# Transposing pairs of 16-bit integers as fp32 words in phase 2 of a decoder layer

## The reference, cut to what matters

```python
def _act_quant(x):
    scale = 127.0 / jnp.clip(jnp.max(jnp.abs(x), axis=-1, keepdims=True), EPS)
    xq = jnp.clip(jnp.round(x * scale), -128.0, 127.0) / scale
    return x + jax.lax.stop_gradient(xq - x)
...
def _bitlinear(x, w):
    return jnp.einsum('bsh,oh->bso', _act_quant(x), _weight_quant(w))
gate = jax.nn.silu(_bitlinear(x, w_gate))
up = _bitlinear(x, w_up)
return _bitlinear(gate * up, w_down)
...
x = _layernorm(x + _L0_attn_ref(x, L0_attn_w_q, L0_attn_w_k, L0_attn_w_v, L0_attn_w_out), axis=-1)
x = _layernorm(x + _L0_xattn_ref(x, ctx_4096, L0_xattn_weight), axis=-1)
x = _layernorm(x + _L0_ffn_ref(x, L0_ffn_w_gate, L0_ffn_w_up, L0_ffn_w_down), axis=-1)
```

## Time and profile before

| | us |
|---|---|
| three runs | 1411.53, 1415.58, 1416.80 |
| median | 1415.58 |
| the profiled execution's own time | 1411.78 |
| its span | 1410.0 |
| phase 2, from the first L717 at 850.98 | 559 |
| one turn of the loop in phase 2 | 34.4 |

### The profile page before, as it was taken

One profiled execution on the slowest core, in us unless ns is written; L12 is line 12 of the kernel. 1 busy time (PEld: TensorE's weight loads), 2 busy tenths in 40 slices (PEclk: granted clock), 3 DMA queues, 4 the chain that ended last, 5 costly groups with the idle time before them and its releaser, 6 DMA issues. The chain is left out here.

```text
span 1410.0 us, 23306 instructions
## 1 busy us (share of the span) xinstructions
PE 1365.8 (97%) x7560; PEld 690.9 (49%) x7560; DVE 1056.1 (75%) x1851; ACT 623.7 (44%) x1209; POOL 217.0 (15%) x262
## 2 busy tenths in 40 slices
PE   8889999999999999999999989999999999999996
PEld 3344555545545554554554544444444444444443
DVE  4996456446577777868867768888888888888884
ACT  7876474455455545545544542332222232223221
POOL 0003213121131321312222221000000000000000
PEclk9999999999999999999999999999999999999999
DMA  9515454445435354453443583222222222222200
GB/s 375 223 61 181 137 186 143 168 132 182 142 111 177 137 160 141 147 178 113 159 159 124 134 278 111 76 75 74 74 74 74 74 74 74 74 74 74 77 27 16
DMA packets 63732, 178.92 MB, mean 127 GB/s; under 512 B 15392, under 2 KB 26832, under 8 KB 63696
## 3 DMA queue, kind: packets, MB, share of 16 engines
q1 hardware_dynamic: 63696, 178.48, 39.2%
HBM read 153.02 MB, written 25.43 MB: 127 GB/s over the span
## 5 line engine op out<-in xcount | busy, mean ns | idle before, releaser
L512 PE MATMUL ps<-weights,xT 128*128 128x512 f16 x2112 | 472.7, 381 | 7.0 <-ACT v L776 6.3
L512 PEld LDWEIGHTS ps<-weights,xT 128*128 128x128 f16 x2112 | 204.4, 98 | 243.1 <-issue 14.2
L717 PE MATMUL ps<-weights 128*128 128x512 fp8e4 (+1 forms) x1536 | 300.0, 357 | 0.0
L717 PEld LDWEIGHTS ps<-weights 128*128 128x128 bf16 x1536 | 146.7, 98 | 155.0
L512 PE MATMUL ps<-weights 128*128 128x512 f16 x768 | 168.9, 379 | 1.1 <-DVE weights L1165 0.6
L745 PE MATMUL ps<-weights 128*128 128x512 fp8e4 x704 | 157.9, 381 | 0.0
L972 ACT ACTIVATE weights<-ps,xscale 128x512 f32<-128x512 f32 x96 | 61.7, 643 | 175.7 <-PE ps L717 175.7
L832 ACT ACTIVATE prob<-prob,negmax,undo 128x128 f32<-128x128 f32 x256 | 122.7, 482 | 8.1 <-DVE negmax L1197 8.0
L512 PEld LDWEIGHTS ps<-weights 128*128 128x128 f16 x768 | 74.9, 98 | 91.8 <-DVE weights L1165 1.6
L745 PEld LDWEIGHTS ps<-weights 128*128 128x128 bf16 x704 | 67.8, 98 | 76.5 <-issue 1.1
L1529 POOL TENSOR_TENSOR rstd<-rstd,expo 128x1 f32<-128x1 f32 x32 | 17.8, 557 | 524.5 <-DVE rstd L1094 524.5
(11 more groups left out here) (162 smaller groups left out, 1791.0 us busy)
## 6 DMA issues: line engine op xcount, KB each, us to landing
wch<-w_ffn SPq DMA_DIRECT2D x96, 688.0 KB, 4.3
wch<-sim_scratch SPq DMA_DIRECT2D x96, 128.0 KB
ternary_scratch<-tern SPq DMA_DIRECT2D x48, 172.0 KB, 1.9
ctx<-ctx SPq DMA_DIRECT2D x16, 512.0 KB
wo_raw<-x_scratch SPq DMA_DIRECT2D x16, 512.0 KB, 3.3
out<-k SPq DMA_DIRECT2D x16, 512.0 KB, 2.7
x_in<-xT_in SPq DMA_DIRECT2D x15, 512.0 KB, 6.9
weights<-x SPq DMA_DIRECT2D x15, 512.0 KB, 10.7
```

Source lines behind the costliest of these rows:

```text
L512: ins = nc.tensor.matmul(ps[:, bank], partsT[:, a, t], weights[:, t, w, half * HALF:(half + 1) * HALF], start=(t == 0 and a + w == 0), sto ...
L717: ins = nc.tensor.matmul(ps[:, 2 * w + a, 0:n], xqT[:, t], w8m[:, t, at:at + n], start=(t == 0), stop=(t == KT - 1))
```

## The change

- The integers are held in fp16 with 512 added (`LIFT`), so that two of them side by side are an fp32 word; the subtraction of 512 and the clip at -128 are done in the copy out of PSUM.
- Two neighbouring columns are transposed together as one fp32 word: `xq_T` issues 4 transposes of 128x128 fp32 in place of 8 in bf16, those of h are 11 in place of 22. They use `idf`; `idb` and its copy at the start are gone.
- A transposed word holds the values of columns 2p and 2p+1 in one place, so the weights are loaded with two neighbouring rows of the matrix in one partition (`gate8_pairs`, `up8_pairs`, `down8_pairs`). The matmuls themselves are as before.
- The copies from PSUM take the even and then the odd halves of the words: they read 16-bit elements with a step of two and write `xqT` and `hT` without gaps.
- The transposes of h go to three banks (4, 5 and 3) in groups of 4, 4 and 3 words' tiles, so that none waits for a bank of its own turn; there are three copies, of 1024, 1024 and 768 elements, in place of 768, 768, 640 and 640. The down product waits for the first at tile 0, for the second at tile 8 and for the third at tile 16.

```diff
-HT_USES = ((0, 6), (6, 12), (12, 17), (17, 22))
-HQ_NEEDS = [-(-min(hi * P, I) * 4 // I) for _, hi in HT_USES]
+JT = IT // 2
+LIFT = 512.0
+HT_USES = ((0, 4), (4, 8), (8, JT))
+HQ_NEEDS = [-(-min(hi * 2 * P, I) * 4 // I) for _, hi in HT_USES]
...
-        TH, AC = 4, 6
+        TH, AC = (4, 5, 3), 6
...
-                    for m, w8m in enumerate((gate8, up8)):
-                        src = tern_dram[m * WCH:(m + 1) * WCH].rearrange("r p n -> (r p n)").rearrange("(k p n) -> p k n", p=P, n=I)
-                        for t in (0, 4):
-                            sp.dma_start(w8m[:, t:t + 4].bitcast(U8), src[:, t:t + 4]).then_inc(ffn_in, 16)
+                    for m, w8m in enumerate((gate8_pairs, up8_pairs)):
+                        src = tern_dram[m * WCH:(m + 1) * WCH].rearrange("r p n -> (r p n)").rearrange("(j p m) -> p j m", p=P, m=2 * I)
+                        for j in (0, 2):
+                            sp.dma_start(w8m[:, j:j + 2].bitcast(U8), src[:, j:j + 2]).then_inc(ffn_in, 16)
...
-                bank = ps[:, 2].bitcast(BF16)
-                for t in range(KT):
-                    ins = nc.tensor.transpose(bank[:, t * P:(t + 1) * P], xq[:, t * P:(t + 1) * P], idb[:])
+                for j in range(KT // 2):
+                    ins = nc.tensor.transpose(ps[:, 2, j * P:(j + 1) * P], rope_c[:, j * P:(j + 1) * P], idf[:])
...
                 for u, (lo, hi) in enumerate(HT_USES):
-                    w = u % 2
-                    if not (isinstance(i, int) and i == 0 and u < 2):
-                        pe.wait_ge(trh_free[w], i * 2 + u // 2)
                     pe.wait_ge(hq_ready, i * 4 + HQ_NEEDS[u])
...
-                    if t in (0, 12):
-                        for w in range(2):
-                            pe.wait_ge(trh_free[w], i * 2 + (1 if t == 0 else 2))
-                        apart(pe)
+                    for u, (lo, _) in enumerate(HT_USES):
+                        if t == 2 * lo:
+                            pe.wait_ge(trh_free[u], i + 1)
+                            apart(pe)
...
-                nc.vector.tensor_scalar(xq, xrnd, MAGIC, 127.0, ALU.subtract, ALU.min).then_inc(xq_ready, 1)
+                nc.vector.tensor_scalar(xq, xrnd, MAGIC - LIFT, 127.0 + LIFT, ALU.subtract, ALU.min).then_inc(xq_ready, 1)
...
-                nc.vector.tensor_scalar(xqT, ps[:, 2].bitcast(BF16).rearrange("p (t n) -> p t n", n=P), -128.0, None,
+                src = ps[:, 2].bitcast(F16).rearrange("p (j n e) -> p j e n", n=P, e=2)
+                nc.vector.tensor_scalar(xqT.rearrange("p (j e) n -> p j e n", e=2), src, LIFT, -128.0, ALU.subtract,
                                         ALU.max).then_inc(pair_free[1], 1)
...
-                    src = ps[:, TH + w].bitcast(BF16)[:, 0:(hi - lo) * P].rearrange("p (t n) -> p t n", n=P)
-                    nc.vector.tensor_scalar(hT[:, lo:hi], src, -128.0, None, ALU.max).then_inc(trh_free[w], 1)
+                    dve.wait_ge(trh_full[u], i + 1)
+                    src = ps[:, TH[u]].bitcast(F16)[:, 0:(hi - lo) * 2 * P].rearrange("p (j n e) -> p j e n", n=P, e=2)
+                    dst = hT[:, 2 * lo:2 * hi].rearrange("p (j e) n -> p j e n", e=2)
+                    nc.vector.tensor_scalar(dst, src, LIFT, -128.0, ALU.subtract, ALU.max).then_inc(trh_free[u], 1)
```

More of the change, by code:

```diff
@@ L95, in decoder @@
         idf = sb("idf", [P, P], F32)
-        idb = sb("idb", [P, P], BF16)
         expo = sb("expo", [P, 2, 9], F32)
@@ L128, in decoder @@
         down8 = w8[:, 2 * KT * I:2 * KT * I + IT * D].rearrange("p (k n) -> p k n", k=IT)
+        gate8_pairs = w8[:, 0:KT * I].rearrange("p (j m) -> p j m", j=KT // 2)
+        up8_pairs = w8[:, KT * I:2 * KT * I].rearrange("p (j m) -> p j m", j=KT // 2)
+        down8_pairs = w8[:, 2 * KT * I:2 * KT * I + IT * D].rearrange("p (j m) -> p j m", j=JT)
         hbuf = over(over_out, I)
-        hq = over(over_out, IT * P // 2).bitcast(BF16)
+        hq_pairs = over(over_out, IT * P // 2)
+        hq = hq_pairs.bitcast(F16)
         hT = over(over_out, IT * P // 2).bitcast(BF16).rearrange("p (t n) -> p t n", n=P)
@@ L189, in decoder @@
         xres_last = wo_raw[:].rearrange("p a n -> p (a n)")[:, D + 2:2 * D + 2]
-        xq = rope_c[:].bitcast(BF16)
+        xq = rope_c[:].bitcast(F16)
         xrnd = xT[:].rearrange("p a t n -> p (a t n)").bitcast(F32)
@@ L281, in decoder @@
         hq_ready = sem("hq_ready")
-        trh_full = [sem("trh_full0"), sem("trh_full1")]
-        trh_free = [sem("trh_free0"), sem("trh_free1")]
+        trh_full = [sem(f"trh_full{u}") for u in range(len(HT_USES))]
+        trh_free = [sem(f"trh_free{u}") for u in range(len(HT_USES))]
         var2_ready = sem("var2_ready")
@@ L431, in turn @@
                         sp.wait_ge(pj_full[w], pj_uses(B - 1, 5) + 1)
-                    for m, w8m in enumerate((gate8, up8)):
-                        src = tern_dram[m * WCH:(m + 1) * WCH].rearrange("r p n -> (r p n)").rearrange("(k p n) -> p k n", p=P, n=I)
-                        for t in (0, 4):
-                            sp.dma_start(w8m[:, t:t + 4].bitcast(U8), src[:, t:t + 4]).then_inc(ffn_in, 16)
[L436 to L441, removed]
+                    for m, w8m in enumerate((gate8_pairs, up8_pairs)):
+                        src = tern_dram[m * WCH:(m + 1) * WCH].rearrange("r p n -> (r p n)").rearrange("(j p m) -> p j m", p=P, m=2 * I)
+                        for j in (0, 2):
+                            sp.dma_start(w8m[:, j:j + 2].bitcast(U8), src[:, j:j + 2]).then_inc(ffn_in, 16)
+                    src = tern_dram[2 * WCH:3 * WCH].rearrange("r p n -> (r p n)").rearrange("(i m) -> i m", m=2 * D)
+                    full = (JT - 1) * P
+                    src_j = src[0:full].rearrange("(j p) m -> p j m", p=P)
+                    for lo, hi in ((0, 3), (3, 7), (7, JT - 1)):
+                        sp.dma_start(down8_pairs[:, lo:hi].bitcast(U8), src_j[:, lo:hi]).then_inc(ffn_in, 16)
+                    sp.dma_start(down8_pairs[0:I // 2 - full, JT - 1].bitcast(U8), src[full:I // 2]).then_inc(ffn_in, 16)
                 if has_next and not has_next2:
@@ L726, in turn2 @@
                 for u, (lo, hi) in enumerate(HT_USES):
-                    w = u % 2
-                    if not (isinstance(i, int) and i == 0 and u < 2):
-                        pe.wait_ge(trh_free[w], i * 2 + u // 2)
                     pe.wait_ge(hq_ready, i * 4 + HQ_NEEDS[u])
[L731 to L734, removed]
+                    for j in range(lo, hi):
+                        ins = nc.tensor.transpose(ps[:, TH[u], (j - lo) * P:(j - lo + 1) * P], hq_pairs[:, j * P:(j + 1) * P], idf[:])
+                    ins.then_inc(trh_full[u], 1)
                 if not (isinstance(i, int) and i == 0):
@@ L1422, in _ @@
             dve.wait_ge(const_in, 64)
-            nc.vector.tensor_copy(idb[:], idf[:]).then_inc(set_up, 1)
             first_rope(0)
@@ L1471, in turn2 @@
                         st.wait(s)
-                    nc.vector.tensor_scalar(hquarter(a, hq), hquarter(a), MAGIC, 127.0, ALU.subtract, ALU.min) \
+                    nc.vector.tensor_scalar(hquarter(a, hq), hquarter(a), MAGIC - LIFT, 127.0 + LIFT, ALU.subtract, ALU.min) \
                         .then_inc(hq_ready, 1)
                 for u, (lo, hi) in enumerate(HT_USES):
-                    w = u % 2
                     if u == 2 and has_next:
@@ L1547, in turn @@
                     pool.wait_ge(sims_ready, b)
-                    nc.gpsimd.memset(down8[64:P, IT - 1], 0.0).then_inc(padded, 1)
+                    nc.gpsimd.memset(down8_pairs[I // 2 - (JT - 1) * P:P, JT - 1], 0.0).then_inc(padded, 1)
                     pool.wait_ge(padded, 1)
```

1 line of the change is left out of this document (removed).

## The result

The changed kernel takes 1435.54 us (median of 4 runs, 1433.80 to 1435.97) against 1413.81 of before (4 runs, 1411.53 to 1416.80): ratio **1.0153, interval 1.0138 to 1.0168**, so 1.5% slower and clear of the noise. The profiled execution took 1435.39 us with a span of 1433.6, 23.6 more than the span of before. Phase 2 begins at 851.20 (850.98 before), so the loss lies in phase 2.

What follows compares the result with a forecast made beforehand. PE sets the pace, and DVE's chain from h to x has no slack. Fifteen turns at +1.42 us give +21.3, the last turn -0.3, sum +21.0: 1432.8 from the profiled execution, 1436.6 from the median; forecast 1435, range 1430 to 1442.

Steps and rivals of the forecast that it cites:

- What bounds: Phase 2 turn of 34.40 us: PE busy 34.08, waiting before the down product and for the next block's x.
- The chain: DVE from the integers of h to those of x: two slower copies +1.32 us, third +0.07, PE's transposes of x +1.39.
- The copy's time: DVE copies from PSUM at a step of two: 1.21 us for 1024 elements, 0.95 us for 768.
- Start of the down product: One slow copy in place of two fast ones: first weights at 1116.14 against 1116.18, nothing won.
- The new waits: Down product at tiles 8 and 16: second and third copies done 2.4 and 1.9 us before PE needs them.
- Behind the chain: From the transposes of x to the next gate matmul: copy's slack used up, 0.2 us more, turn +1.42 us.
- The transposes of x: Four fp32 transposes take 0.44 us against 0.59 for eight bf16 ones, saving 0.15 us of PE on the path.
- The last turn: Only the first copy precedes the down product, which starts at 1391.32 against 1391.61: -0.3 us.
- The signs: Profile after: 1024-element copies about 1210 ns, turn 35.8 us, PE idle about 1.4 us before transposes of x, clock 1.00.
- The copies keep two elements a step: Rival at L1481 and L1150: copies of 0.691 and 0.55 us, about 1411, or 1408 to 1417 us; chance 0.09.
- The clock: Rival: a 1.4 us wait each turn lowers PE's clock, 36 us more, 1469 us; chance 0.03.
- Slower still: Rival: a copied element takes more than one step, 1.79 us a copy, 3.6 a turn, 1466 us; chance 0.03.

Runs made afterwards that it cites:

- the new order: Kernel before with bf16 transposes, three banks and DVE's copies of h moved to where DVE waits: 1408.82 us, ratio 0.9964.
- tried alone: Kernel before with bf16 transposes and plain copies, groups of 8, 8 and 6 tiles in three banks, down product waiting group by group: 1414.14 us.
- the run that counted on it: Changed kernel with plain copies and the new order, 1407.37 us, compared with the new order on bf16 transposes, 1408.82 us.
- the kernel with plain copies: Changed kernel with all copies of h and x without gaps, PE's weight loads taking the step of two: 1414.27 us, ratio 1.0007.
- the kernels with copies of 4.8 us: Changed kernel with copies reading without gaps and writing SBUF in scattered pieces: rows of two elements 1667.54 us, rows of four 1668.85 us.

## Why the prediction was right, point by point

- **What bounds.** PE sets the pace and waits at two places, of which the second, DVE's chain from the integers of h to those of x, has no slack. Right, and shown twice: lengthening it lengthens the turn, and shortening it (the new order) makes the kernel before faster. "No slack" is 0.20 us too strict: it compared L1146 with the load at 1124.24, but the matmuls of the transposes started at 1124.44. The chain is 1.43 us longer, the matmuls came 1.24 later.
- **The copy's time.** 1.21 us taken, 1.220 to 1.224 measured; 0.95 and 0.948 for 768. The number held, but its argument did not, and that it held is luck: with plain reading and a step on the writing side the words are read once, and the copy takes 1.29 us. The price of 1024 words read and that of one element a step happen to be the same.
- **Start of the down product.** Nothing won: +0.02 us. One slow copy takes what two fast ones took.
- **The new waits.** Covered, as the sum had it, and without cost when tried alone.
- **The chain.** +1.39 forecast, +1.43 at L1146. The third copy put L1099 0.86 us behind it, 0.87 forecast.
- **Behind the chain.** +1.42 in all forecast, 1.55 to 1.57 measured. The term most at fault is the lag behind the copy of x: its end (1137.51 + 1.22 = 1138.73) to the first gate matmul (1138.88) is 0.15 us, where 0.06 were taken. Behind L1146 the lag is 0.06 here too (1136.75 to 1136.81), so it was carried over from a place where it holds to one where it doesn't; why it is longer there stays open. It makes 1.4 us in fifteen turns, and with the chain's 0.04 it is the whole 2 us that the turns fell short. DVE still waited 0.23 us for L1489, where none was forecast; nothing hung on it.
- **The transposes of x.** "Saves 0.15 us of PE" is wrong. The 0.59 us for eight in the earlier trace rows were read from weight loads, which ran ahead while matmuls of the down product were still going; on PE itself eight in bf16 take 0.45 and four in fp32 0.44. The copy did start 0.15 us earlier behind the first load, but because PE was idle when the load came. A right shift for a wrong reason; the run that counted on it (3 to 4 us for pairs) missed.
- **The last turn.** -0.3 forecast. From the integers to the first load of the down product it took 3.00 us (1414.96 - 1411.96) against 3.26 (1391.61 - 1388.35), so -0.26 there. But nothing of it arrived: from the same integers to the end of the down product it is 13.97 us against 13.93, and to the end of the span 21.64 against 21.65. In both kernels PE comes out of a wait of 3.7 us or more, and the granted clock is 0.50 in the two microseconds from 1415 and from 1391. In the changed kernel the loads go at their slow spacing of 0.43 us until 5.54 us behind the integers, before until 5.07. 0.47 us more at half the clock cost about as much as the earlier start had won. The rows after, then before:

```profile
1411.96 1.79 DVE L1472 TENSOR_SCALAR weights<-weights 128x688 f16<-128x688 f32 x4
...
1414.96 0.14 PEld L745 LDWEIGHTS ps<-weights 128*128 128x128 bf16 x2 [0.82 <-issue]
1414.99 10.94 PE L745 MATMUL ps<-weights 128*128 128x512 fp8e4 x44 [0.57 <-issue]
...
1417.50 7.93 PEld L745 LDWEIGHTS ps<-weights 128*128 128x128 bf16 x37 [0.28 <-issue]
```

```profile
1388.35 1.79 DVE L1472 TENSOR_SCALAR weights<-weights 128x688 bf16<-128x688 f32 x4
...
1391.71 10.57 PE L745 MATMUL ps<-weights 128*128 128x512 fp8e4 x44
...
1393.42 8.36 PEld L745 LDWEIGHTS ps<-weights 128*128 128x128 bf16 x39 [0.28 <-issue]
```

- **The total.** 1435 forecast, 1435.54 measured, and that they agree this closely is luck too. The spans of the profiled executions differ by 23.6 us, where 21.0 were forecast: the turns were 0.13 us short each, and the last turn gave nothing. The medians differ by 21.7.
- **The signs.** Copies of 1210 ns were named, 1220 to 1224 came; a turn of 35.8 us, 35.95. Of PE's idle time about 1.4 us were forecast ahead of the transposes of x; there are 1.09 there and 0.60 ahead of the down product. The sum does not name the latter, but it only takes the place of the third and fourth group of transposes.
- **The rivals.** "The copies keep two elements a step" was priced at 1411, or 1408 to 1417, with -0.2 to +0.13 us a turn; the kernel with plain copies has +0.10 and 1414.27. The clock stayed at 1.00 in the turn with its wait of 1.09 us. In the kernels with copies of 4.8 us, where PE waits up to 4.1 us at a time, the mean granted clock of the run is 0.92 against 0.99; that rival had its place, but not here. "Slower still" took 1.79 us for a copy, where its 1.6 ns an element make 1.64; nothing hung on it.

## What to carry to other kernels

Look at what a cheaper operation hands to the next one: halving the transposes moved the unpacking into copies on an engine whose chain had no slack. If interleaved 16-bit data must come apart, let the reader do it that can at no cost (here PE's weight load at a step of two), and keep a step of one on both sides of a VectorE copy of 16-bit elements. And when a chain is the bound, put its movable steps where that engine waits for others: this, with two copies given to an idle engine, was worth 11 us between the profiled executions and 15 between the medians, where the transposes were worth none.

## What the runs showed of the hardware that was not expected

- A copy of 16-bit elements from PSUM to SBUF (1024 per partition): 0.686 us with a step of one on both sides, also when read in rows of two with gaps between them; 1.22 with a step of two in reading; 1.29 with a step of two in writing; 4.8 when each element is written 128 or 256 elements from the last.
- A transpose of 128x128 takes 0.11 us of PE in fp32 and 0.056 in bf16: per byte the same.
- A load of 128 bf16 columns at a step of two takes the same 98 ns as one without gaps (660 loads of L747 with all copies plain; 622 of L745 in the changed kernel).
